# Routing of the first expert layer moved inside the first attention, sequence by sequence

## What is computed

```
x = x + attention0(layernorm(x))            # 16 heads of 16, rotary mix, causal softmax
y = layernorm(x);  logits = y @ gate_w      # 8 experts
top_w, top_idx = top_k(logits, 2);  top_w = softmax(top_w)
x = x + sum over the two experts: top_w * (gelu(y @ w1[e] + b1[e]) @ w2[e] + b2[e])
```

## Time and profile before

| | |
|---|---|
| median of 3 runs | 2752.2 us (2752.0 to 2756.41) |
| profiled execution | 2746.9 us, span 2745.2 us, granted clock 0.942 |
| PE busy | 2419.3 us, 88% |
| DVE busy | 1799.5 us, 66% |
| ACT busy | 1342.6 us, 49% |
| POOL busy | 824.5 us, 30% |

### The profile page before, as it was taken

One profiled execution on the slowest core, in us unless ns is written; L12 is line 12 of the kernel. 1 busy time (PEld: TensorE's weight loads), 2 busy tenths in 40 slices (PEclk: granted clock), 3 DMA queues, 4 the chain that ended last, 5 costly groups with the idle time before them and its releaser, 6 DMA issues. The chain is left out here.

```text
span 2745.2 us, 53741 instructions
## 1 busy us (share of the span) xinstructions
PE 2419.3 (88%) x20524; PEld 2156.7 (79%) x20524; DVE 1799.5 (66%) x3223; ACT 1342.6 (49%) x2061; POOL 824.5 (30%) x1226
## 2 busy tenths in 40 slices
PE   4999999953599999935788898789999999999999
PEld 3666666632599999924677787689999999999999
DVE  7666666664488888849998888267444454544544
ACT  1555555631377777633444453344454554545454
POOL 4555566317200000055677766410000000000000
PEclk7899999976799999967899999989999999999999
DMA  9995000003477677747656565144222222222222
GB/s 302 332 334 169 2 2 2 2 6 126 156 241 238 234 230 240 220 131 181 154 148 156 152 168 147 40 138 143 91 90 86 83 89 88 86 89 87 89 78 87
DMA packets 195374, 373.31 MB, mean 136 GB/s; under 512 B 28964, under 2 KB 105960, under 8 KB 194152
## 3 DMA queue, kind: packets, MB, share of 16 engines
q1 hardware_dynamic: 185816, 343.31, 40.7%
q0 software_dynamic: 9360, 27.27, 3.0%
HBM read 336.95 MB, written 100.66 MB: 159 GB/s over the span
## 5 line engine op out<-in xcount | busy, mean ns | idle before, releaser
L2314 DVE TENSOR_TENSOR e_h_lo<-e_h,e_h_hi 128x512 fp32r<-128x512 f32 x320 | 222.0, 694 | 300.2 <-ACT e_h_hi L2390 300.2
L2452 PE MATMUL e_h_ps<-e_yT_hi,e_w_hi 128*128 128x256 f32 x1280 | 362.9, 283 | 3.0 <-ACT e_h L2376 2.2
L2468 PE MATMUL e_y_ps<-e_w_hi,e_h_hi 128*128 128x256 f32 x1280 | 359.1, 281 | 2.4 <-DVE e_h_lo L2314 2.3
L2452 PE MATMUL e_h_ps<-e_yT_hi,e_w_lo 128*128 128x256 f32 x1280 | 358.7, 280 | 0.0
L2452 PE MATMUL e_h_ps<-e_yT_lo,e_w_hi 128*128 128x256 f32 x1280 | 358.7, 280 | 0.0
L2468 PE MATMUL e_y_ps<-e_w_lo,e_h_hi 128*128 128x256 f32 x1280 | 355.7, 278 | 0.0
L2468 PE MATMUL e_y_ps<-e_w_hi,e_h_lo 128*128 128x256 f32 x1280 | 355.7, 278 | 0.0
L2390 ACT ACTIVATE e_h_hi<-e_h 128x512 fp32r<-128x512 f32 x320 | 202.2, 632 | 276.7 <-DVE e_h L2309 220.5
L2376 ACT ACTIVATE e_h<-e_h_ps,e_b 128x512 f32<-128x512 f32 x320 | 218.9, 684 | 175.0 <-PE e_h_ps L2452 151.3
L2309 DVE TENSOR_TENSOR e_h<-e_h,e_spread 128x512 f32<-128x512 f32 x256 | 176.8, 691 | 133.5 <-ACT e_h L2376 132.4
L462 DVE TENSOR_REDUCE a_top<-a_ring 128x2 f32<-128x1024 f32 (+3 forms) x256 | 204.2, 819 | 72.2 <-PE a_ring L651 70.8
(11 more groups left out here) (371 smaller groups left out, 6772.6 us busy)
## 6 DMA issues: line engine op xcount, KB each, us to landing
e_w<-in_w SPq DMA_DIRECT2D x78, 1024.0 KB, 5.6
e_spread<-share_store SPq DMA_DIRECT2D x512, 128.0 KB, 2.8
a_keys<-rows_store SPq DMA_DIRECT2D x128, 256.0 KB, 5.0
a_queries<-rows_store SPq DMA_DIRECT2D x86, 256.0 KB, 4.9
a_running_hidden<-rows_store SPq DMA_DIRECT2D x42, 256.0 KB, 4.7
e_xs<-sorted_x SPq DMA_DIRECT2D x39, 256.0 KB, 5.1
sorted_y<-e_ys POOLq DMA_DIRECT2D x39, 256.0 KB, 5.9
e_stage_buf<-in_w_all SPq DMA_DIRECT2D x10, 512.0 KB, 3.9
```

Of the source, the lines that this page charges most:

```text
L2314: dve.tensor_tensor(h_parts[q % 2][1][:, :], h[:, q % 2, :], h_parts[q % 2][0][:, :], ALU.subtract).then_inc(h_lo.sem, h_lo.tick())
L2452: last = pe.matmul(h_ps[q % 2][:, cols], l, r, start=(m == 0), stop=(m == len(ops) - 1))
L2468: last = pe.matmul(y_ps[n][:, 0:D], h_parts[q % 2][a][:, n * P:(n + 1) * P], w2[b][:, c, :], start=(q == 0 and m == 0), stop=(q == CH - 1 ...
```

## The change

1. The block of routing keeps only what needs all counts. The rest is done inside the attention for one sequence at a time, the one before the running one, by new units in `BETWEEN`: statistics `S0` and scale with guess `S1` (after `b1` of pair 3 and `b0` of pair 4), normalise `N`, turn `U`, logits `L`, turn back `T`, choices `C0` and `C1`, ranks `K`, placing `W`. `U`, `L`, `T` and `K` take a ring buffer each. The last sequence goes through the same functions at the end of the attention.
2. POOL refines a sequence's inverse root between the third and the fourth tile of a stack, and stores a sequence's rows (8 indirect DMAs) behind `add_bias`. For the last two sequences both follow the loop.
3. The normalised rows of one sequence lie in the memory of `qk` tiles 2 and 3. So `N` waits for the running stack and for the last stores, and `p2` for the stores.
4. `stack_tile` has 8 operations instead of 13, over wider operands.
5. SP clears `sorted_x` first, which the first stores wait for, then `sorted_y` in copies of half the size, each awaited. Three small loads move to the attention's start.

```diff
         BETWEEN = {("b1", 0): ("x",), ("b0", 1): ("p0",), ("b1", 1): ("p1",), ("b2", 1): ("p2",), ("b0", 2): ("p3",),
-                   ("b1", 2): ("t",), ("b2", 2): ("y",), ("a2", 1): ("n",)}
+                   ("b1", 2): ("t",), ("b2", 2): ("y",), ("a2", 1): ("n",),
+                   ("b1", 3): ("S0",), ("b0", 4): ("S1",), ("b1", 5): ("N",), ("b0", 6): ("U",), ("b1", 6): ("L",),
+                   ("b2", 6): ("T",), ("b0", 7): ("C0",), ("b1", 7): ("C1",), ("b2", 7): ("K", "W")}
...
+            for e in range(2):
+                engine.tensor_tensor(pairs_of(turned[:, :])[:, :, :, :, e], pairs_of(qk[:, n])[:, :, :, :, 1 - e],
+                                     mix[:, :, :, :, e].broadcast_to([P, 2, H0, DH0 // 2]), ALU.mult).then_inc(step.sem, step.tick())
             engine.wait_ge(step.sem, step.at(step.n, turn))
+            engine.tensor_tensor(qk[:, n], qk[:, n], rope[:, n].unsqueeze(2).broadcast_to([P, 2, H0, DH0]),
+                                 ALU.mult).then_inc(step.sem, step.tick())
+            engine.wait_ge(step.sem, step.at(step.n, turn))
+            twice = lambda ap: ap.unsqueeze(2).broadcast_to([P, H0, 2, DH0])
+            engine.tensor_tensor(q_stack[m][:, n, :, 0:2 * DH0].rearrange("p h (u d) -> p h u d", u=2), twice(qk[:, n, 0]),
+                                 twice(turned[:, 0]), ALU.add).then_inc(step.sem, step.tick())
+            engine.tensor_tensor(k_stack[m][:, n, :, 0:4 * DH0].rearrange("p h (u two d) -> p h u two d", u=2, two=2)[:, :, :, 0],
+                                 twice(qk[:, n, 1]), twice(turned[:, 1]), ALU.add).then_inc(step.sem, step.tick())
+            engine.wait_ge(step.sem, step.at(step.n, turn))
+            engine.tensor_tensor(qk[:, n], qk[:, n], turned[:, :], ALU.add).then_inc(step.sem, step.tick())
...
+            def refine_rows(q):
+                pool.wait_ge(y_step.sem, y_step.at(2 * TB + 5, q))
+                y_refined.n = 0
+                rsqrt_refine(pool, y_refined, q, y_rstd[:, :], y_half[:, :], y_newton[:, :], g.three_halves[:, :])
+
+            def scatter(q):
+                if q == 0:
+                    pool.wait_ge(zeros_spread.sem, ZERO_SPREADS * 16)
+                for k in range(2):
+                    pool.wait_ge(rows_ready.sem, rows_ready.at(k + 1, q))
+                    for n in range(TB):
+                        row = q * TB + n
+                        pool.indirect_dma_start(
...
             for s in range(1, B):
-                stack(s, s % 2, range(TB))
+                turn_step.n = stacked.n = 0
+                for n in range(TB):
+                    stack(s, s % 2, n)
+                    if n == 2 and s >= 2:
+                        refine_rows(s - 2)
                 turn_step.close()
                 add_bias(s)
                 if s == 1:
                     refine(2)
+                else:
+                    scatter(s - 2)
+            for s in (B - 2, B - 1):
+                refine_rows(s)
+                scatter(s)
...
+            def normalise(q):
+                dve.wait_ge(y_refined.sem, y_refined.at(12, q))
+                if q + 2 < B:
+                    dve.wait_ge(stacked.sem, stacked.at(2 * TB, q + 2))
+                if q:
+                    dve.wait_ge(written.sem, written.at(0, q))
...
             low_att(B - 1, 0)
             add_proj(B - 1, 1)
+            row_statistics(B - 1)
+            row_scale(B - 1)
+            normalise(B - 1)
+            low_rows(B - 1, 2)
+            take_logits(B - 1, 1)
+            choose(B - 1, 0)
+            choose(B - 1, 1)
+            place_rows(B - 1, 2)
...
+            def find_logits(q, k):
+                pe.wait_ge(yT_lo.sem, yT_lo.at(KC, q))
+                split_product(ring[k][0:E0, 0:S], [((gate_hi[:, c, :], gate_lo[:, c, :]), (xnT_hi[:, c, :], xnT_lo[:, c, :]))
+                                                   for c in range(KC)]).then_inc(gates_done.sem, gates_done.tick())
```

More of the change, by code:

```diff
@@ L205, in attention0_phase @@
         block = ctx.enter_context(nc.Block())
[L207 to L216, removed]
-            engine.wait_ge(step.sem, step.at(step.n, turn))
[L218 to L224, removed]
@@ L272, in _, with spread @@
             for at in range(0, TOKENS, step):
-                sp.dma_start(t["sorted_x"][at:at + step, :].rearrange("(n p) d -> p n d", p=P), zeros).then_inc(zeroed.sem,
+                sp.dma_start(t["sorted_y"][at:at + step, :].rearrange("(n p) d -> p n d", p=P), zeros).then_inc(zeroed.sem,
                         zeroed.tick(16))
             sp.wait_ge(zeroed.sem, zeroed.at(zeroed.n))
[L276 to L282, removed]
+            def spread(name, at, size, behind):
+                dst, src = (t[rows][a:a + size, :].rearrange("(p r) d -> p (r d)", p=P)
+                            for rows, a in ((name, at), ("sorted_y", 0)))
+                sp.dma_start(dst, src).then_inc(behind.sem, behind.tick(16))
+            END = BLOCKS * SLOT_TOKENS
+            for at in range(0, END, TOKENS):
+                spread("sorted_x", at, min(TOKENS, END - at), zeros_spread)
+            sp.wait_ge(zeros_spread.sem, zeros_spread.at(zeros_spread.n))
+            for at in range(TOKENS, END, TOKENS // 2):
+                spread("sorted_y", at, min(TOKENS // 2, END - at), spread_zeros)
+                sp.wait_ge(spread_zeros.sem, spread_zeros.at(spread_zeros.n))
         @block.gpsimd
@@ L290, in refine, with stack @@
                 rsqrt_refine(pool, refined, None, rstd[:, a:b], half[:, a:b], newton[:, a:b], ones[:, a:b])
[L292 to L297, removed]
+            def stack(s, m, n):
+                pool.wait_ge(qkv_taken.sem, qkv_taken.at(2 * n + 1, s))
+                stack_tile(pool, n, m, turned, turn_step, stacked, s)
             def add_bias(s):
@@ L311, in prepare @@
                 refine(1)
-                stack(0, 0, range(TB // 2))
+                for n in range(TB // 2):
+                    stack(0, 0, n)
                 pool.wait_ge(stat_step.sem, stat_step.at(PREPARED))
@@ L444, in _ @@
                     norm(s)
+                if what == "S":
+                    (row_statistics, row_scale)[r](s)
+                if what == "N":
+                    normalise(s)
+                if what == "U":
+                    low_rows(s, k)
+                if what == "T":
+                    take_logits(s, k)
+                if what == "C":
+                    choose(s, r)
+                if what == "K":
+                    rank_unit = k
+                if what == "W":
+                    place_rows(s, rank_unit)
                 if what == "x":
@@ L782, in _ @@
         def _(pool):
[L783 to L804 removed]
+            pool.wait_ge(g.written.sem, g.written.at(0, B))
         @block.vector
```

439 lines of the change are left out of this document (194 added, 245 removed).

## The result

The changed kernel takes 2796.97 us (median of 4 runs, 2795.76 to 2797.77), the kernel before 2752.1 beside it: 1.0162 times as long, 95% interval 1.0144 to 1.0179. The change makes it slower by 44.9 us, 1.6%. In the profiled executions the span went from 2745.2 to 2796.1 us, +50.9.

The account below looks back on a forecast made before the run. PE was taken to bound the attention, POOL issuing stores the routing stage. Terms -76.4 - 1.5 + 47 (PE and DVE work) + 37 (stall) + 30 (clock) = +36 us; stated 2788 us, own range 2765 to 2812, full range 2722 to 2835.

Parts of the forecast that it names:

- The removed stage: Routing between attention and experts: shrinks to the last sequence and what needs all counts, 76.4 us gained.
- 0.4 for the next block: Removed stage: time from POOL issuing its last store to the routing block's opening, 0.4 us.
- The new PE work: Attention, per sequence: added transposes, products, turns and rank products on PE, 3.25 us with no cover.
- The POOL stall: Between stack tiles three and four: refinement waits for DVE's scale, PE stands 6.1 us in six stacks, 37 us.
- DVE in step 7: Last pair of a sequence: choices and placing overload DVE, so PE gives back 3.9 us a sequence.
- Its share of the clock: Half clock after PE's waits in the last pair: 1.5 us lost each, 9 of the clock's 30 us.
- the last one: Seventh sequence's routing in the attention, with no maxima behind it: 4 us.
- +0.5 (start): Kernel start: two tiles stacked by POOL with shorter operation lists, some 1.5 us gained.
- The faster one: Rival: POOL's refinement never holds PE, so stall and clock loss go, 2721 us; chance 0.18.
- The stall without the clock: Rival: PE stops but resumes at 2.4 GHz, or last-pair waits are absorbed, 2758 us; chance 0.15.
- The clock stays low until dense products come: Rival: after each stall only the next qkv products restore the clock, 78 us more, 2866 us; chance 0.10.
- The contention: Rival: DVE's statistics, scale and normalisation run at half speed beside POOL, 3.5 us a sequence, 2809 us; chance 0.10.

Follow-up runs that it names:

- e_scale_early: Changed kernel with DVE's statistics behind b0 and scale behind b1 of pair 3: 1.0014 of the kernel before, median 2753.0 us.
- e_refine_last: Changed kernel with POOL refining the routed sequence's scale behind the fourth tile instead of between third and fourth: 1.0085 of the kernel before, 2776.18 us.
- e_shift: e_refine_last with turn, logits, turn back and both choices one or two places earlier in the pairs: 1.0062 of the kernel before, 2766.68 us.
- e_both: Changed kernel with the edits of e_scale_early and e_refine_last together: 1.0076 of the kernel before, 2772.37 us.
- e_spread: e_both with the places of e_shift and the placing behind b1 of the next sequence's pair 0: 1.0102 of the kernel before, 2782.68 us.
- e_short_ops: e_refine_last with POOL's four 512-element operations a tile each split in two of 256: 1.0085 of the kernel before, 2776.03 us.
- e_pause: e_both with two POOL waits added, for DVE's scale before the fourth tile and for normalised rows before the bias: 1.0085 of the kernel before.
- e_pause_spread: e_spread with the same two POOL waits as e_pause: 1.0095 of the kernel before.
- e_pause_w: e_pause with only the placing moved behind b1 of the next sequence's pair 0: 1.0157 of the kernel before.
- e_quiet: e_scale_early with POOL's bias addition waiting until DVE has normalised the routed rows: 1.0022 of the kernel before.
- e_late_rank: e_quiet with ranks and placing behind b0 of the next pair 0 and each choice one operation shorter: 0.9991 of the kernel before, 2752.38 us.
- e_stack_alone: Kernel before with only the eight-operation stack_tile, no routing moved: 0.9995 of the kernel before.

## Why the prediction was right, and where it was off

**One sum for the sequences, and how well it fits.** For one sequence of each kernel, PE's waits are from its timeline and the time at the lower clock from the stretches. The last column is what 64.2 us of before plus the predicted 3.25 us of new PE work, plus the waits, leave over, divided by the low time:

```
kernel          period   waits   low clock   rest per us of low clock
before           64.20    0.4       0
changed          81.92    8.3      20.5        0.30
e_scale_early    75.13    4.9       6.8        0.41
e_refine_last    78.63    4.7      17.0        0.38
e_shift          79.36    5.1      17.3        0.39
e_both           78.57    6.1      13.7        0.37
e_spread         78.35    7.4      10.2        0.34
e_short_ops      79.41    8.0      13.7        0.29
e_pause          78.96    5.4      13.6        0.45
e_pause_spread   78.49    6.9      10.2        0.41
e_pause_w        84.37    9.0      18.2        0.44
e_quiet          75.05    5.1       6.8        0.37
e_late_rank      73.29    4.5       3.4        0.39
```

By the median of these, a microsecond at 1.2 GHz costs some 0.4 us. In the changed kernel it is 0.30, since 4.1 of its 20.5 us lie inside the stall, where PE does nothing. The sequences of one kernel are not all alike. Over the full sequences of these traces with 6.8 us or more at the lower clock the last column goes from 0.23 to 0.51, so the sum is good to some 1 to 3 us a sequence. `e_late_rank` has no steady period: its five full ones are 75.0, 74.7, 73.3, 75.7 and 77.3, and the table has the shortest. The sum was made after the runs and is a fit. Its one test, the forecast for `e_late_rank`, missed by 12 us or more: other waits of about the size of those it took away stand in its trace. The sum does not say how long the clock stays low.

**The removed stage.** Predicted 56.8 us, measured 60.0. The first store came 21.8 us after the last addition (21.4 predicted), eight stores took 9.8 (10.1), the two uncovered loads 2.9 (3.3). The term that failed is "0.4 for the next block": it opened 5.6 us after the last store was issued, because POOL, at the start of the routing block, waits until the stores have landed. All that follows the two loads took 19.9 us and not 21.6.

**The new PE work.** Predicted 3.25 us a sequence. With it the last column comes out near 0.4 both at low times of 3.4 to 6.8 us and at 17, so it holds within about half a microsecond. No run measured it alone.

**The POOL stall.** Predicted 6.1 us, six times, measured 5.4, six times, at the place named: refinement waits (5.6 predicted, 4.43 measured), then 3.35 and 8.4 us (3.4 and 8.3). `e_scale_early` shows by experiment that the place of the scale made it.

**DVE in step 7.** Predicted 3.9 us, measured 2.2 of waits there and 0.7 at two other places. Its share of the clock was undersized: 1.5 predicted, but the second half-clock spell has 10 us of busy PE, some 4 by the rate above. The first was oversized, 3.5 against some 2.4. Together 6.2 against 5.0. That the six sequences come out within 3.6 us of the forecast is in part luck: the waits of the stall and of step 7 were 1.7 us a sequence shorter than forecast, and the clock cost 1.2 more.

**Beyond the six sequences.** I gave the last one 4 us; the remainder is 12.7. In that stretch (619.5 to 647.7) some 24 us are at the lower clock. And I gave nothing to what follows: the experts and all behind them took 6.0 us more. 4.3 of these lie in the expert block itself, whose second products take 281 ns in the median instead of 277. That goes with the change: the median is 281 in the changed kernel and in all eleven experiments that route in the attention, 277 in the kernel before and 276 in `e_stack_alone`. Why is open.

Sum of the misses: +0.5 (start), -3.6 (six sequences, 106.4 for 110), +8.7 (last sequence), +3.2 (stage), +6.0 (behind it): 14.8, the difference between +36 and +50.9. The forecast's own range was drawn narrower than its terms: their bounds add up to -67 and +62 us around it, 2721 to 2850, where it has 2765 to 2812 without saying why.

**The rivals.** The faster one stated that it decides at 6.1 us of earlier scale. `e_scale_early` takes most of that away, and the stall and most of its clock go; but new waits stand where DVE's work now meets PE, so it ends at 2753, not at 2721. "The stall without the clock" is refuted by the rows at 0.50. "The clock stays low until dense products come" is refuted too: it came back in every sequence before the next qkv products. The contention was priced as a slowdown of one half, 3.5 us a sequence. What the runs show is a stand until POOL's operation has ended. In the changed kernel it cost little, because POOL stood idle during the scale and the normalisation's 3.08 us (1.38 unhindered) lay behind the stall. But in `e_refine_last`, `e_shift`, `e_both`, `e_spread` and `e_short_ops` an operation so held stands ahead of the wait of PE for the maxima that comes back in each sequence, of up to 1.9 to 4.0 us; and my sentence that the median speaks against it looked at the wrong thing: what counts is whether the one operation that PE waits for meets POOL's.

## What to carry to other kernels

Where the engine that bounds a stage has no idle time, every wait added to it is paid, and with the clock it was paid 1.3 to 2.4 times over in the kernels of the table: work moved under its cover must arrive early on every engine, by its own path, and not on average. Before two engines that work on the same memory are both kept busy, look whether a small operation that others wait for meets a long one of the other engine, and compare their ends. Adding up the gains of single edits failed here: in `e_both` one edit took away the pause that had made the other work, and in `e_quiet` PE reached the next late result sooner. So look for that next one first.

## What was not expected of the hardware

Small TENSOR_SCALAR and SCALAR_TENSOR_TENSOR operations of DVE from SBUF to SBUF stood until POOL's running operation had ended, 1.06 to 1.25 us for work of 0.17, within 0.03 us of its end, while those with a PSUM operand and the statistics ran on. PE's waits of 0.66, 0.73 and 0.79 us in step 7 were followed by 10.2 us at 1.2 GHz in the changed kernel and in `e_both`, and by 3.4 us in `e_scale_early` and `e_refine_last`: the same waits, and three times as long at the lower clock. And ACT stood 1.85 us and PE 1.0 us, with nothing in the trace that explains it, while POOL issued indirect stores, in one order of the program and not in another.
